# Routed experts of a four-layer network on one core: stationary gate and up weights copied to a fixed place, products made turned

## The reference, cut to what matters

```
topk_scores, topk_idx = top_k(softmax(flat @ router_w.T + router_bias), 4)
h = silu(einsum('nd,ehd->neh', flat, gate_w)) * einsum('nd,ehd->neh', flat, up_w)     # 32 experts, 128 hidden
expert_out = einsum('neh,edh->ned', h, down_w)
out = (sel(expert_out, topk_idx) * topk_scores).sum(axis=1)
out = out + silu(flat @ sgate_w.T) * (flat @ sup_w.T) @ sdown_w.T                     # one shared expert, 512 hidden
```

## Time and profile before

| | us |
|---|---|
| median of three executions | 1504.26 |
| lowest and highest | 1490.34 and 1516.75 |
| profiled execution, its own time | 1502.2 |
| its span | 1500.4 |
| mean granted TensorE clock | 0.885 of full |
| first turn_in to the start of line 893 | 1266.97 to 1451.54 |

### The profile page before, as it was taken

How to read it: one execution, slowest core, us unless ns; L and a number is a source line. 1 busy time by engine, 2 the same in 40 slices (tenths; PEclk the granted TensorE clock), 3 DMA queues, 4 the chain that set the end, 5 groups by cost and what they waited for, 6 DMA issues and landing times.

```text
span 1500.4 us, 19335 instructions
## 1 busy us (share of the span) xinstructions
PE 1267.0 (84%) x6360; PEld 774.8 (52%) x6361; DVE 721.5 (48%) x2083; ACT 437.0 (29%) x833; POOL 285.5 (19%) x306
## 2 busy tenths in 40 slices
PE   5999999999347799999998758999678797899983
PEld 3534434434234244444443548999555455777762
DVE  7363563463974245565464540111266652455446
ACT  2222222222052235454443302333233210233320
POOL 2111111000122000000000040111112662355550
PEclk9999999999677689999996868999866799999996
DMA  9999994000010000000000374555309223345436
GB/s 313 339 336 332 328 335 146 0 0 0 19 39 1 0 1 1 1 1 1 31 1 1 117 238 152 176 183 189 110 27 352 85 88 91 116 147 150 145 123 259
DMA packets 140424, 186.75 MB, mean 124 GB/s; under 512 B 8672, under 2 KB 124896, under 8 KB 140224
## 3 DMA queue, kind: packets, MB, share of 16 engines
q1 hardware_dynamic: 130800, 159.28, 34.2%
q0 software_dynamic: 9552, 26.52, 4.8%
HBM read 83.71 MB, written 102.06 MB: 124 GB/s over the span
## 4 chain that ended last, share of the span: by engine, by line
PE 61%; DVE 14%; issue 6%; DMA 5%; POOL 5%; SPq 4%; ACT 4%; another core or an unknown queue 0%; DVEq 0%; POOLq 0%; ACTq 0%
PE psum L1886 13%; PE psum L1214 6%; PE psum L2078 6%; PE psum L1225 5%; POOL xs L872 3%; PE psum L2134 3%; DMA xs<-xn,arena 3%; DVE arena L2677 2%; PE psum L2111 2%; PE psum L1879 2%; PE psum L2064 2%; PE psum L2158 2%; SPq L957 2%; PE psum L1914 2%; SPq L958 2%
## 5 line engine op out<-in xcount | busy, mean ns | idle before, releaser
L1886 PE MATMUL psum<-arena 128*128 128x512 f32 x432 | 205.8, 628 | 0.0
L2677 DVE TENSOR_REDUCE arena<-psum 128x4 f32<-128x616 f32 x128 | 102.2, 798 | 128.8 <-PE psum L2078 127.5
L1886 PEld LDWEIGHTS psum<-arena 128*128 128x128 f32 x432 | 83.6, 200 | 120.4 <-issue 119.6
L2078 PE MATMUL psum<-arena 32*128 32x308 f32 x512 | 114.0, 525 | 24.2 <-DVE arena L2677 22.9
L1142 POOL DMA_INDIRECT ys<-xnT,arena x96 | 92.4, 962 | 114.2 <-DVE xnT L1108 92.0
L2252 ACT ACTIVATE arena<-psum,arena 128x512 f32<-128x512 f32 x72 | 49.1, 686 | 173.5 <-PE psum L1886 161.0
L2370 ACT ACTIVATE arena<-psum 128x2048 f32<-128x2048 f32 x40 | 75.0, 1875 | 79.2 <-PE psum L2115 60.6
L1785 POOL TENSOR_TENSOR x_tok<-x_tok,add_row 128x1024 f32<-128x1024 f32 x16 | 37.7, 2365 | 293.4 <-ACT xn L1688 163.8
L1002 PE MATMUL psum<-arena,xn 128*128 x384 | 89.9, 388 | 1.4 <-ACT xn L1053 0.9
L2078 PEld LDWEIGHTS psum<-arena 32*128 32x128 f32 x512 | 42.6, 203 | 93.2 <-DVE arena L2677 61.9
L1214 PEld LDWEIGHTS psum<-side,arena 128*128 128x128 f32 x736 | 87.4, 195 | 2.7 <-ACT side L1259 1.6
(11 more groups left out here) (397 smaller groups left out, 2111.5 us busy)
## 6 DMA issues: line engine op xcount, KB each, us to landing
xs<-zeros SPq DMA_DIRECT2D x8, 8576.0 KB, 59.7
arena<-in_W SPq DMA_DIRECT2D x31, 1024.0 KB, 11.9
xn<-xs SPq DMA_DIRECT2D x96, 134.0 KB
arena<-in_gate_up SPq DMA_DIRECT2D x4, 2048.0 KB, 16.2
arena<-ys SPq DMA_DIRECT2D x4, 2048.0 KB, 14.6
arena<-in_down SPq DMA_DIRECT2D x4, 1024.0 KB, 15.5
xs<-zeros SPq DMA_DIRECT2D x1, 2990.0 KB, 16.8
side<-xs SPq DMA_DIRECT2D x23, 130.0 KB
```

The lines of the kernel that those rows point to most:

```text
L1886: ins = pe.matmul(bank[dict(hn=4, r=5, z=6, xn=7)[k]][:], lhs[:, cols], r, start=(start and n == 0), stop=(stop and n == len(w) - 1))
L2078: ins = pe.matmul(bank[4 + i][:, 0:2 * M].rearrange("p (h m) -> p h m", h=2), qhT[rows, n % 3, c, t * P:(t + 1) * P], keys[rows, l, c, b, ...
L2677: dve.tensor_reduce(neg[:, n % 2, t, 2 * pair:2 * pair + 2, 2 * c:2 * c + 2], psum[:, 4:6, 0:2 * M].rearrange("p b (h m) -> p b h m", h=2) ...
```

## The change

The hidden products exchange their operands. For each of the four tiles and for gate and up apart, an expert's 128 weight columns are the stationary operand and the turned tokens (128 columns) the moving one, so that the result comes out turned, hidden by token: 16 products of 128 columns in place of 8 of 256. `turn_hidden`, `copy_hidden`, `qhidT` and their semaphores go. The stationary operand is at a fixed address: ScalarE copies the four experts' 512 columns each from `arena` into the new double buffer `qweight` (`copy_weights`), with the register load of the expert word and the computed addresses on ScalarE. TensorE keeps a register load for the down weights; it now stands between turn_in(q + 2) and output(q). The gate and up banks are 2 and 3 for even quads and 4 and 5 for odd ones. `qtanh` and `qhid` move to other columns.

```
+            def hidden(q, u):
                 pe.wait_ge(*inT_ready.at(7, 2 * q + 2))
+                pe.wait_ge(qweight_ready, q + 1)
+                for t in range(4):
+                    for w, dst in enumerate(quad_banks(u)):
+                        for c in range(C):
+                            ins = pe.matmul(dst[:, t * P:(t + 1) * P],
+                                            qweight[:, u, t, c * 2 * F4 + w * F4:c * 2 * F4 + (w + 1) * F4],
+                                            qinT[:, u, c, t * P:(t + 1) * P], start=(c == 0), stop=(c == C - 1))
                 ins.then_inc(hidden_done.sem, 1)
-            def turn_hidden(q, u):
...
             def output(q, u, experts, first=False):
                 if not first:
                     pe.wait_ge(*out_ready.at(7, q))
-                pe.wait_ge(qhidT_ready, q + 1)
+                pe.wait_ge(qhid_ready, q + 1)
...
+            def step(q):
                 u = q % 2
-                ahead = experts_of(q + 1)
-                hidden(q + 1, 1 - u, ahead)
+                hidden(q + 1, 1 - u)
                 turn_in(u, q // 2 + 1)
-                output(q, u, now, q == 0)
-                turn_hidden(q + 1, 1 - u)
+                output(q, u, experts_of(q), q == 0)
...
+            def copy_weights(q, u):
+                word = act.value_load(route[7]["expert"][0:1, bass.ds(q, 1)], min_val=0, max_val=E4 ** 4 - 1)
+                if q >= 2:
+                    act.wait_ge(*hidden_done.at(7, q - 1))
+                for t in range(4):
+                    e = (word >> (5 * t)) & (E4 - 1)
+                    ins = act.activation(qweight[:, u, t], arena[:, bass.ds(e * (C * 2 * F4) + GU0, C * 2 * F4)], ACT.Copy)
+                ins.then_inc(qweight_ready, 1)
+            act.wait_ge(*expert_ready.at(7, 1))
+            act.wait_ge(w7_loaded, 8 * 16)
+            copy_weights(0, 0)
             copy_in(0, 0)
+            copy_weights(1, 1)
             tanh_gate(0, 0)
             copy_in(1, 1)
-            copy_hidden(0, 0)
             for q in range(NQ - 2):
                 u = q % 2
+                copy_weights(q + 2, u)
                 tanh_gate(q + 1, 1 - u)
                 copy_in(q + 2, u)
-                copy_hidden(q + 1, 1 - u)
             tanh_gate(NQ - 1, 1)
-            copy_hidden(NQ - 1, 1)
```

More of the change, by code:

```diff
@@ L282, in build @@
         qout = xnT[:].rearrange("p u c n -> p (u c n)").rearrange("p (u n) -> p u n", u=2)
-        qtanh = arena[:, 4096:5120].rearrange("p (u t n) -> p u t n", u=2, t=4)
-        qhid = arena[:, 5120:6144].rearrange("p (u t n) -> p u t n", u=2, t=4)
-        qhidT = arena[:, 6144:7168].rearrange("p (u n) -> p u n", u=2)
+        qtanh = xq[:].rearrange("p u n -> p (u n)").bitcast(F32).rearrange("p (u n) -> p u n", u=2)
+        qhid = arena[:, 7168:8192].rearrange("p (u n) -> p u n", u=2)
+        qweight = arena[:, 2172:2172 + 8 * C * 2 * F4].rearrange("p (u t n) -> p u t n", u=2, t=4)
         gathered7 = arena[:, GU0:GU0 + T * K4 * D].rearrange("p (t k d) -> p t k d", t=T, k=K4)
@@ L504, in build @@
         (shares_shifted, shares_exp, shared_hid, shared_done, shared_added, shared_down, shared_tanh, qtanh_ready,
[L505 removed]
+         qgate_ready, qhid_ready, qweight_ready, w7_loaded) = (
             sem(k) for k in ("shares_shifted", "shares_exp", "shared_hid", "shared_done", "shared_added", "shared_down",
[L507 removed]
+                             "shared_tanh", "qtanh_ready", "qgate_ready", "qhid_ready", "qweight_ready", "w7_loaded"))
         ws_loaded = sem("ws_loaded")
@@ L951, in shared_vector, with quad_banks @@
             shared_add_vector(dve, last // 4 - 1)
+        def quad_banks(u):
+            return (bank[2], bank[3]) if u == 0 else (bank[4], bank[5])
         def quads_sync(sp):
@@ L996, in turn_in @@
                     ins.then_inc(in_turned.sem, 1)
-            def hidden(q, u, experts):
+            def hidden(q, u):
                 pe.wait_ge(*inT_ready.at(7, 2 * q + 2))
[L1000 to L1005, removed]
-                ins.then_inc(hidden_done.sem, 1)
-            def turn_hidden(q, u):
[L1009 to L1012, removed]
+                pe.wait_ge(qweight_ready, q + 1)
[5 more added lines that the diff above has]
+                                            qinT[:, u, c, t * P:(t + 1) * P], start=(c == 0), stop=(c == C - 1))
+                ins.then_inc(hidden_done.sem, 1)
             def output(q, u, experts, first=False):
@@ L1016, in output @@
                     pe.wait_ge(*out_ready.at(7, q))
-                pe.wait_ge(qhidT_ready, q + 1)
+                pe.wait_ge(qhid_ready, q + 1)
                 for t, e in enumerate(experts):
-                    ins = pe.matmul(bank[6 + t // 2][:, (t % 2) * D:(t % 2 + 1) * D], qhidT[:, u, t * P:(t + 1) * P],
+                    ins = pe.matmul(bank[6 + t // 2][:, (t % 2) * D:(t % 2 + 1) * D], qhid[:, u, t * P:(t + 1) * P],
                                     arena[:, bass.ds(e * D + DOWN0, D)], start=True, stop=True)
                 ins.then_inc(out_done.sem, 1)
-            def step(q, now):
+            def step(q):
                 u = q % 2
-                ahead = experts_of(q + 1)
-                hidden(q + 1, 1 - u, ahead)
+                hidden(q + 1, 1 - u)
                 turn_in(u, q // 2 + 1)
-                output(q, u, now, q == 0)
-                turn_hidden(q + 1, 1 - u)
-                return ahead
+                output(q, u, experts_of(q), q == 0)
             pe.wait_ge(w7_loaded, 8 * 16)
@@ L1035, in quads_tensor @@
             pe.wait_ge(shared_hid, 4 * (G - 1))
-            now = experts_of(0)
-            hidden(0, 0, now)
+            hidden(0, 0)
             turn_in(1, 0)
-            turn_hidden(0, 0)
             pe.wait_ge(shared_added, 2 * (G - 1))
             for q in range(NQ - 2):
[L1042 to L1047, removed]
+                step(q)
+            hidden(NQ - 1, 1)
+            output(NQ - 2, 0, experts_of(NQ - 2))
+            output(NQ - 1, 1, experts_of(NQ - 1))
         def quads_scalar(act):
@@ L1056, in tanh_gate @@
                 act.wait_ge(*hidden_done.at(7, q + 1))
[L1057 to L1062, removed]
+                act.activation(qtanh[:, u], quad_banks(u)[0], ACT.Tanh, scale=0.5).then_inc(qtanh_ready, 1)
+            def copy_weights(q, u):
[9 more added lines that the diff above has]
+            copy_weights(0, 0)
             copy_in(0, 0)
+            copy_weights(1, 1)
             tanh_gate(0, 0)
             copy_in(1, 1)
-            copy_hidden(0, 0)
             for q in range(NQ - 2):
                 u = q % 2
+                copy_weights(q + 2, u)
                 tanh_gate(q + 1, 1 - u)
                 copy_in(q + 2, u)
-                copy_hidden(q + 1, 1 - u)
             tanh_gate(NQ - 1, 1)
-            copy_hidden(NQ - 1, 1)
         def quads_vector(dve):
-            up = psum[:, 2:4].rearrange("p b (t w n) -> p (b t) w n", t=2, w=2)[:, :, 1]
-            gate = psum[:, 2:4].rearrange("p b (t w n) -> p (b t) w n", t=2, w=2)[:, :, 0]
             def hidden(q, u):
+                gate, up = quad_banks(u)
                 dve.wait_ge(qtanh_ready, q + 1)
```

1 line of the change is left out of this document (removed).

## The result

The changed kernel takes 1535.32 us (median of 4, 1529.54 to 1540.4) where the kernel before takes 1504.72 us on the same chip (1490.34 to 1516.75): ratio 1.0217, 95% interval 1.0174 to 1.026. It is some 31 us slower, outside my range of 1490 to 1520. The profiled execution took 1540.4 us.

What follows compares the result with a forecast made beforehand. The loop feeding TensorE (turning, output, copy_out, select, SyncE load, DMA) was taken as the bound. Terms -1.3 + 0 + 1.0 + 0.8 - 0.9 = -0.4 gave 1501.8, 1503.9 on the median's scale; forecast 1503.5 us, range 1490 to 1520.

Steps and rivals of the forecast that it cites:

- SP and POOL: SyncE and GpSimd queues in the quads: nothing added; SyncE's slowdown, 4.62 to 5.84 us a load, stays unchanged.
- What is late next when copy_hidden goes is nothing: Tanh and gating in the quads: output(q) waits for a gating made a whole step earlier, so no new delay.
- Rival C: ScalarE becomes the bound of the quads if its register work slows by 1.2 to 2.3 us: 1519 us, chance 0.08.
- The copies: ScalarE's four weight copies a quad: 2.9 us at most, covered by 1.2 us, cost 0.
- Rival D: TensorE's clock stays at 1.2 GHz in the quads because of more short DMA waits: 1619 us, chance 0.03.
- The saving of TensorE: Products and transposes in the quads: 0.34 us a quad saved, 0.4 with register work; mostly lengthens TensorE's wait.
- the load round: Two-quad loop of turning, output, copy_out, select, SyncE load and DMA: 14.63 us, taken to set the quad time.
- 7 turnings of 0.4 us halved: Turnings that did not wait for the DMA: each gives at most 0.4 us, half counts, so -1.3 us.
- Rival B: TensorE's address work causes SyncE's slowdown and mostly goes, leaving TensorE the bound: 21 us off, 1483 us, chance 0.03.
- The start: First quad: ScalarE copies weights before its input copies, delaying the products; +0.8 us, ends -0.5 and +3.5.
- The moved register load: TensorE's register load, now between turning and output, enters the round: +0.1 us in each of 10 rounds, +1 us.
- the end: After the last load, the hidden products of quads 22 and 23 and the gating lose 0.4 us each: -0.9 us.

Runs made afterwards that it cites:

- the narrow: Changed kernel with all four scatters of a quad kept but each row 16 columns long instead of 256: 1534.74 us, ratio 1.020.
- the few scatters: Changed kernel with only one or two of a quad's four scatters kept: 1485.34 us with one, 1486.89 us with two.
- the ledger: Comparison of the changed kernel's 24 quads with four scatters and with one: 218.5 against 168.5 us, idle ahead of the products 35.8 against 2.9 us.
- the changed kernel with one scatter: Changed kernel with three of a quad's four scatters left out: 1485.34 us, ratio 0.987.
- the selection experiment: Kernel before with VectorE's select of quad q+2 put ahead of copy_out of quad q: 1511.51 us, ratio 1.005.
- the version in pairs: Changed kernel with a quad's third scatter held until the products of quad q+2, or until the first two landed: 1508.47 and 1505.22 us.

## Why the prediction was wrong

**The step that failed** is under "SP and POOL": "I take this slowdown as tied to the scatters and unchanged." The first half was right, and the narrow and the few scatters show it. But the rows held more than SyncE's slowdown. In the earlier trace rows the output's 2.83 us already had a late signal in it, for TensorE's own output takes 1.89. I took it for a constant of the output step. It is a property of a stretch of time, from 2 to 4 us behind the first scatter's start (where in this span differs from row to row) to 1.0 us behind the fourth one's end, and it hits nearly every signal that falls in it. The change moved the signals against the scatters, and 69.6 us of lateness behind the turnings (1.4 before) came of it: "unchanged" didn't hold. Why they came to lie just there, a shorter quad or the missing turn_hidden, no run parts.

**"What is late next when copy_hidden goes is nothing"** was right of the output and blind for the rest. The turning has a single reader on the path, ScalarE's copy, and that has no cover, no other work of TensorE between the signal and the need of it: the next products wait at once. That costs the 32.9 us of the ledger.

**Rival C** had the sign and half the size (1519), but its cause was wrong. The copies are no dearer than I had them, four in 2.19 us where I took 2.9, and their register load takes 276 ns, 285 at most: ScalarE's register work was not slowed as SyncE's is, which C had supposed. **Rival D**, the clock, was argued away with one idle of 3.04 us that the clock outlasted. That no new wait would be as long was true of most (2.28 us in the quad above), and the clock fell all the same, in nine pieces behind the start, which cost the products some 14.5 us. One idle time that left the clock alone bounds nothing. The Trainium skill, "TensorE: Matmul & The Clock Gate", section "HAM oscillation — how this bites in real kernels", warned of bursts parted by waits, and here the trace agrees in part (clock 0.50 in 1329.5 to 1332.8): the products of nine of the 24 quads were slowed and not of every one, and the waits were for a semaphore and not for a DMA.

**What came true.** The saving of TensorE, 0.34 to 0.4 us a quad, was measured as 6.73 - 6.28 = 0.45, with TensorE as the bound of both. The 32 passes hold TensorE for 3.57 us there, as forecast (from 1342.27 to the next turning at 1345.84 in the changed kernel with one scatter). That something else than TensorE bounds the kernel before fits its 7.32 us a quad against 6.73 without most scatters; the runs don't part the load round from the late signals in it. (In the sum, 7 turnings of 0.4 us halved are 1.4 and not 1.3, which changes nothing.) My belief in the selection experiment, that freeing the round alone would gain, failed for the same reason as the forecast. Rival B's time (1483) is that of one scatter, 1485, but not for its reason. **The start**: the products of quad 0 end at 1279.5 instead of 1275.5, but 2.4 of these 4 us had passed before the first turning, which starts at 1269.35 instead of 1266.97. From there it is 10.17 against 8.54 us, 1.6 us longer, where I took 0.8 and had 3.5 as the end; TensorE was idle longer there while ScalarE copied weights. The moved register load took 325 ns in the median; it, and the end, can't be told apart from the rest.

## What to carry to other kernels

Before a forecast, find which signals of the trace arrive late (a reader starting 1 us or more behind its producer, "remote") and what runs at that time; then ask of each changed phase which signals will fall there, and which of them have cover. In this kernel indirect scatters from GpSimd are cheap in ones and twos and dear in rows of four and more (three were not tried): hold the third until the first two have landed, even though it adds a wait. And order the work so that between each signal and TensorE's need of it stands one other piece of TensorE's work.

## What the runs showed of the hardware

- While four indirect DMAs follow one another on GpSimd (0.96 us each, one every 1.26 us), TensorE's semaphore signals are held back, up to 3.3 us in the changed kernel, and most are let go some 1.0 us behind the last one's end. One or two in a row hold back next to nothing (at most 0.83 us). SyncE's instructions go on in steps of 0.7 us while four run (0.69 us in the kernel before), and in a row of eight TensorE's passes do as well. Which part of the chip they share isn't settled by these runs.
- The bytes of a scatter don't matter between 16 and 256 columns (957 and 959 ns on GpSimd, ratio 1.020 and 1.022). The Trainium skill, "Perfetto Trace Analysis", section "DMA Instruction — SWDGE (GPSIMD)", says that such a row ends when the descriptors are made, not when the data have moved. The trace agrees: rows of 0.96 us, and a landing 3.3 us or more after the issue, as this row of the version in pairs has it (least, median, most, over all DMAs that write or read `ys`, the last gather among them):
```profile
DMA to landing us min/median/max: 3.3/7.4/21.7
```
- One idle time of 3.04 us of TensorE left the clock at its 2.4 GHz level (kernel before), and others of 2.28 us were followed by the 1.2 GHz level (changed kernel).
